# Vision-transformer block: attention's side work moved to other steps, and 56 expert units of 512 slots with gathered weights

## The reference

```python
def block(x, W, b, ...):
    h = patches(x) @ W + b                          # 64 images, 196 tokens of 192 (N = 12544)
    # attention, on layernorm(h): 12 heads of 16, rope, causal
    q, k, v = rope(heads(Wq)), rope(heads(Wk)), heads(Wv)
    weights = where(mask, erf(q k / 4) + 1, 0)
    h = h + (weights v / max(weights.sum(-1), 1e-6)) @ Wproj.T
    # experts, on flat = layernorm(h)
    probs = softmax(flat @ Wr)                       # 8 experts
    topk_p, topk_i = top_k(probs, 2), normalised
    order = argsort(-score, axis=1)[:, :3920]        # at most 3920 tokens per expert
    expert_out = (silu(d @ w1) * (d @ w3)) @ w2 * weight      # d = flat[order], inner 768
    routed = zeros.at[order].add(expert_out)
    shared = silu(flat @ s1) * (flat @ s3) @ s2      # all tokens
    return h + routed + shared
```

## Time and profile before

| what | us |
|---|---|
| median of three executions | 3905.7 |
| their range | 3896.83 to 3907.6 |
| profiled execution | 3916.64 |
| its span, first to last instruction | 3914.8 |
| TensorE busy | 3537.2 (90%) |
| VectorE busy | 2483.3 (63%) |
| ScalarE busy | 1703.8 (44%) |
| GpSimd busy | 1427.5 (36%) |
| mean granted TensorE clock (share of 2.4 GHz) | 0.848 |

### The profile page before, as it was taken

The page is one execution under the profiler, slowest core; times in us unless marked ns, Lnnn a source line. Parts: engine busy times, 40 slices in busy tenths (PEclk is TensorE's granted clock), DMA queues, the critical chain, the costliest instruction groups (busy, mean ns, idle before and its releaser), DMA issues. The chain is left out here.

```text
span 3914.8 us, 80584 instructions
## 1 busy us (share of the span) xinstructions
PE 3537.2 (90%) x28468; PEld 2523.2 (64%) x28468; DVE 2483.3 (63%) x4827; ACT 1703.8 (44%) x3390; POOL 1427.5 (36%) x1302
## 2 busy tenths in 40 slices
PE   6989889989999998998923999999999999999998
PEld 5766667767677676776712666666666666666665
DVE  5878778777787777877765555554444455345443
ACT  3444444444454444444401444434444444444443
POOL 1222222222222222222221555215555556555555
PEclk7877778777777777787555999999999999999999
DMA  1011111110110101101011222222332323323222
GB/s 67 31 47 39 39 51 34 43 51 26 51 49 28 51 31 46 51 31 47 24 49 48 63 70 71 67 75 35 61 62 39 60 37 62 62 36 61 39 39 32
DMA packets 166708, 186.21 MB, mean 48 GB/s; under 512 B 45263, under 2 KB 145711, under 8 KB 162319
## 3 DMA queue, kind: packets, MB, share of 16 engines
q1 hardware_dynamic: 95696, 123.03, 9.7%
q0 software_dynamic: 57472, 48.46, 8.3%
q10 hardware_dynamic: 13262, 10.65, 0.8%
HBM read 107.75 MB, written 67.85 MB: 45 GB/s over the span
## 5 line engine op out<-in xcount | busy, mean ns | idle before, releaser
L1235 DVE SCALAR_TENSOR_TENSOR ffn_hidden<-ffn_up,ffn_silu 128x490 f32<-128x490 f32 (+2 forms) x534 | 358.2, 672 | 803.9 <-ACT ffn_silu L1218 735.5
L656 POOL TENSOR_TENSOR weights<-weights,x_pair 128x400 f32<-128x400 f32 x384 | 395.6, 1030 | 1243.3 <-DVE weights L521 669.5
L1218 ACT ACTIVATE ffn_silu<-ffn_gate 128x490 f32<-128x490 f32 (+2 forms) x534 | 311.0, 583 | 700.8 <-PE ffn_up L1186 663.6
L570 DVE RECIPROCAL recip<-x_product 128x200 f32<-128x200 f32 x384 | 535.6, 1395 | 0.0
L1203 PE MATMUL ffn_out<-ffn_w_hi,ffn_hidden_hi 128*126 128x192 f16 (+2 forms) x2124 | 522.5, 246 | 0.0
L1205 PE MATMUL ffn_out<-ffn_w_hi,ffn_hidden_lo 128*126 128x192 f16 (+2 forms) x2124 | 522.4, 246 | 0.0
L1204 PE MATMUL ffn_out<-ffn_w_lo,ffn_hidden_hi 128*126 128x192 f16 (+2 forms) x2124 | 522.3, 246 | 0.0
L1391 POOL DMA_INDIRECT out_rows<-done,kept x256 | 426.6, 1666 | 153.7 <-issue 85.3
L1381 POOL DMA_INDIRECT tokens<-dram_x,ids x256 | 279.8, 1093 | 392.8 <-issue 228.5
L1228 DVE TENSOR_TENSOR ffn_hidden_lo<-ffn_hidden,ffn_hidden_hi 128x490 f16<-128x490 f32 (+2 forms) x534 | 355.4, 665 | 8.8
L740 PE MATMUL bank<-w_tok,patches 128*128 128x192 f32 x1536 | 346.1, 386 | 14.1 <-DVE ident L486 14.1
(11 more groups left out here) (185 smaller groups left out, 8074.4 us busy)
## 6 DMA issues: line engine op xcount, KB each, us to landing
patches<-in_patches SPq DMA_DIRECT2D x32, 1176.0 KB, 5.2
ffn_raw<-in_w SPq DMA_DIRECT2D x18, 768.0 KB
dram_x_t<-x_t SPq DMA_DIRECT2D x32, 392.0 KB, 2.5
x_t<-dram_x_t SPq DMA_DIRECT2D x24, 512.0 KB
base<-dram_h SPq DMA_DIRECT2D x24, 384.0 KB
out_rows<-sums ACTq DMA_DIRECT2D x24, 384.0 KB
v_held<-v SPq DMA_DIRECT2D x64, 102.0 KB, 2.3
dram_h<-h SPq DMA_DIRECT2D x32, 192.0 KB
```

What stands on the lines that cost most here:

```text
L570: nc.vector.reciprocal(recip[:, n % 2], x_product[:, n % 2]).then_inc(inverted, 1)
L656: nc.gpsimd.tensor_tensor(weights[:, n % 4], weights[:, n % 4], x_pair[:, n % 4, ::-1], ALU.mult)\
L1218: nc.scalar.activation(T.silu[:, m % 2, 0:n], T.gate[m % 2][:, 0:n], ACT.Silu, scale=1.0 / (TOKEN_SCALE * WEIGHT_SCALE)).then_inc(T.silued, 1)
L1235: nc.vector.scalar_tensor_tensor(T.hidden[:, m % 2, 0:n], T.up[m % 2][:, 0:n], HIDDEN_SCALE / (TOKEN_SCALE * WEIGHT_SCALE), T.silu[:, m % ...
```

## The change

The diff has two parts that don't touch.

**Attention.** TOK works two units ahead instead of one, with two buffers h_new: turn u makes the tokens of unit u+2. A first turn "pre" with TOK alone is added, and a turn "late" without TOK before the last two. Steps of the side work change (all engines), and the scores of the next unit's first pair move into step 11, ahead of attend. SP loads patches two units ahead, both at the start, and does the v_held copies ahead of the h2 and x2 stores.

**Experts.** A slot table of 56 units of 512, each with one expert: an expert's entries are rounded up to whole units at run time, so its unit count follows from the routing. A table `weights_of` gives each unit's expert. During the first 16 shared units of the loop (8 pairs) each expert's weights are loaded, split, and stored as half-precision rows in DRAM (`front`, 12,288 B per partition; `back`, 4,608 B). For each routed unit GpSimd gathers `front` and `back` by the unit's expert, double buffered.

```diff
-TOK, YT, PROJ, LN1T, QK, VV, X2T, ROUTE, QKT = (
-    (0, 1), (2, 3), (4, 5), (6, 7), (8, 9, 11, 12), (10, 13), (14, 15), (16,), tuple(range(17, 23)))
+LN1T, QK, VV, YT, PROJ, X2T, QKT, ROUTE, TOK = (
+    (0, 1), (2, 3, 4, 5), (6, 9), (7, 8), (10, 11), (13, 14), tuple(range(15, 21)), (22,), (12, 21))
...
# TensorE, attention
                 for n in range(PAIRS):
-                    if pairs:
-                        if n < PAIRS - 1:
-                            scores(kind, u, n + 1, qk_t[slot])
-                        if n >= LAG:
+                    if pairs and n < PAIRS - 1:
+                        scores(kind, u, n + 1, qk_t[slot])
+                    if n == PAIRS - 1 and has_next:
+                        copied(QKT)
+                        scores("first" if kind == "pro" else "mid", u + 1, 0, qk_t[prev])
+                    if pairs and n >= LAG:
...
+                    if n == 3 and has_next:
+                        pe.wait_ge(normed_ready, 4 * u + 8)
+                        transposed(LN1T, normed)
+                        copied(LN1T)
+                    if n in (3, 4) and has_next:
+                        for t in range(2 * n - 6, 2 * n - 4):
+                            out = room(QK[t])
...
+                    if n in (7, 8) and has_tokens:
...
+                        tokens(n - 7)
...
+                    if n == 10 and has_next:
+                        pe.wait_ge(roped, 4 * u + 8)
+                        for g in range(6):
+                            transpose_qk(g)
+                    if n == 11 and has_tokens:
+                        tokens(2)
+                        tokens(3)
+                    if n == 11 and has_prev:
+                        pos = X2T[0]
+                        pe.wait_ge(free[pos % NB], fills(kind, u, pos))
...
# VectorE, attention
+                    if n == 0 and has_next:
+                        norm(0, token_root(u - 1), h_new[prev], normed, normed_ready)
+                    if n == 1 and has_prev:
                         outputs(u - 1, 1)
...
-                    if n in (6, 7) and has_next:
+                    if n in (3, 4) and has_next:
...
+                    if n == 11 and has_tokens:
+                        dve.wait_ge(free[TOK[-1] % NB], fills(kind, u, TOK[-1]))
+                        nc.vector.tensor_tensor(h_new[slot][:], h_new[slot][:], over(bias[:], [128, 4, D]), ALU.add)\
+                          .then_inc(biased, 1)
+                        dve.wait_ge(biased, u + 3)
+                        spread_of(0, h_new[slot])
...
# routing
+            ts(rounded[:], offset[:, 1, E:2 * E], float(XU - 1), None, ALU.add)
+            ts(rounded[:], rounded[:], XU.bit_length() - 1, None, ALU.logical_shift_right)
+            step(nc.vector.tensor_copy(units[:], rounded[:]))
+            step(nc.vector.tensor_tensor_scan(ends[:], ones[:, 0:E], units[:], 0.0, ALU.mult, ALU.add))
...
# experts, SP
             def unit(g, half, slot, tiles, e=None):
...
+                if e is not None and slot == 0:
+
+                    sp.wait_ge(T.weights_lo, 3 * e + 6)
+                    sp.sem_inc(load_spacer, 1)
+                    sp.dma_start(dram["front"][bass.ds(e * 128, 128), :], T.front[1][:]).then_inc(staged, 16)
+                    sp.dma_start(dram["back"][bass.ds(e * 128, 128), :], T.back[1][:]).then_inc(staged, 16)
+                    load_weights(sp, dram, T, e + 1)
...
# experts, GpSimd
+            def routed(v, half, slot):
+                if not among(v, XUNITS - 1):
+
+                    pool.wait_ge(T.gated, MI * (SHARED + v))
+                    pool.sem_inc(spacer, 1)
+                    if not (isinstance(v, int) and v == 0):
+                        pool.wait_ge(back_in[slot], 16 * (half + slot))
+                        pool.sem_inc(spacer, 1)
+                    owned(v + 1, slot)
+                    weights(slot, "front", T.front[slot], front_in[slot])
...
+                nc.gpsimd.tensor_copy(kept[slot][:], ids[slot][:]).then_inc(ids_kept, 1)
...
                     gather(v + 2, half + 1, slot)
...
+                    pool.wait_ge(T.out_full, 2 * (SHARED + v))
+                    pool.sem_inc(spacer, 1)
+                    weights(slot, "back", T.back[slot], back_in[slot])
...
# experts, ScalarE, behind store(g - 1, ...)
+                if e is not None and slot == 1:
+
+                    act.wait_ge(staged, 32 * e + 32)
+                    act.wait_ge(T.raw_in, 48 * e + 96)
                     weights_hi(nc, T, 1)
...
# experts, VectorE
+        if m == 2 and between:
+            between()
...
+                def remainders():
+
+                    dve.wait_ge(T.weights_hi, 3 * e + 6)
+                    weights_lo(nc, T, 1)
```

More of the change, by code:

```diff
@@ L720, in transpose_qk, with tokens @@
                     last.then_inc(full[pos % NB], 1)
-                for n in range(PAIRS):
-                    if pairs:
-                        if n < PAIRS - 1:
-                            scores(kind, u, n + 1, qk_t[slot])
-                        if n >= LAG:
-                            if n == LAG:
-                                pe.wait_ge(held_in[slot], 32 if kind == "first" else 32 * (prior + 1 - slot) + 32)
-                            attend(kind, u, n - LAG, v[slot], v_held[slot])
+                def tokens(n):
+                    pos, at = TOK[n // 2], n % 2 * D
+                    out = room(pos) if n % 2 == 0 else bank[pos % NB]
+                    for i in range(KP):
+                        last = nc.tensor.matmul(out[:, at:at + D], wide(patches[slot], i, n), tok_w[:, i, :],
+                                                start=(i == 0), stop=(i == KP - 1))
+                    if n % 2:
+                        last.then_inc(full[pos % NB], 1)
@@ new lines, in turn @@
+                    if n in (3, 4) and has_next:
+                        for t in range(2 * n - 6, 2 * n - 4):
+                            out = room(QK[t])
+                            product(out[:, 0:2 * D], normed_t, t, qkv_w, 2 * D).then_inc(full[QK[t] % NB], 1)
+                    if n in (4, 5) and has_next:
+                        pos = VV[n - 4]
+                        out = room(pos)
+                        for c in range(2):
+                            last = product(out[:, c * D:(c + 1) * D], normed_t, 2 * (n - 4) + c, qkv_w[:, :, 2 * D:3 * D], D)
+                        last.then_inc(full[pos % NB], 1)
@@ L860, in routing @@
         rank = sb("rank", [128, E])
-        base = sb("base", [128, E])
+        ones = sb("ones", [128, 128])
+        row = sb("row", [128, 1])
+        numbers = sb("numbers", [128, XUNITS])
+        ended = sb("ended", [128, XUNITS, E])
+        owner = sb("owner", [128, XUNITS])
+        rounded = sb("rounded", [128, E], I32)
+        units = sb("units", [128, E])
+        ends = sb("ends", [128, E])
         place = sb("place", [128, E])
@@ L878, in routing @@
         block = ctx.enter_context(nc.Block())
-        constants = ((rank, "rank"), (same, "same"), (before, "before"), (base, "base"))
+        constants = ((rank, "rank"), (same, "same"), (before, "before"), (row, "row"), (numbers, "numbers"))
         @block.sync
@@ L1068, in _ @@
                 ts(slots[:, :, c], best[:], float(SLOTS), None, ALU.add)
+            tt(ended[:], numbers[:].unsqueeze(2).to_broadcast([128, XUNITS, E]),
+               ends[:].unsqueeze(1).to_broadcast([128, XUNITS, E]), ALU.is_ge)
+            step(nc.vector.tensor_reduce(owner[:], ended[:], AX.X, ALU.add))
+            ts(owner[:], owner[:], float(E - 1), None, ALU.min)
+            ts(weights_of[:], owner[:], 128.0, row[:, 0:1], ALU.mult, ALU.add)
 TOKEN_SCALE, WEIGHT_SCALE, HIDDEN_SCALE = 2.0 ** 6, 2.0 ** 6, 2.0 ** 4
```

468 lines of the change are left out of this document (221 added, 247 removed).

## The result

The changed kernel takes 3965.1 us (median of four runs, 3960.68 to 3972.31), against 3901.3 us for the kernel before in the runs beside it. The ratio is 1.017, 95% interval 1.013 to 1.021: it is slower, by 1.7%. The forecast was 3752 us and a range to 3925, so both miss. The profiled execution has a span of 3958.8 us, 44.0 more than before.

A forecast was written before the change was run, and what follows sets the result against it. TensorE was taken as bound in attention, shared and routed units, GpSimd close behind in the last. From 3916.6: attention -180, routing +4, shared +150, short unit -8, routed -120 give 3763, less 10.9 for the median: 3752 us; range 3600 to 3925.

The forecast's parts named there:

- the ids load beside the weights: Routed units, GpSimd's loop: the ids load takes 0.6 us more beside weights, in a loop of 19.7 us.
- rival E: Routed units: GpSimd's loop replaces TensorE as bound, 26 us by dearer weight gathers and later ids; 4050 us, chance 0.12.
- The point of decision of rival E: Routed units: the time per unit from which rival E decides, 23.4 us.
- The x_t term with its clock: Shared units: tokens queued behind 4.3 MB on SP's queue cost 11.5 us per pair, the low clock afterwards 2 us.
- the casts, the remainders and their clock: Shared units with preparation: TensorE loses 2.1 us per pair to ScalarE's casts and 3.2 to VectorE's remainders.
- Rival D: Shared units: SP's queue doesn't hold the tokens, so 13.5 us less for each of 8 pairs; 3644 us, chance 0.12.
- The short unit: End of shared stage: the one preparation beside the short unit goes, saving 8 us.
- Waits: Attention: TensorE's waits of 4.3 us per turn go, as the start of the softmax chain is covered.
- Clock: Attention: 2.0 us less per turn, as 24 token matmuls at the boundary replace idle time.
- The cover of the boundary: Attention, step 11: next turn's scores ahead of attend, with 24 token matmuls and route matmul behind, cover the softmax chain's start.
- Rivals B and C: Attention: B, clock stays high, 48.6 us per turn, 3590, chance 0.15; C, heavy run stays low, 58, 3870, chance 0.15.
- Routing: Routing stage: a memset, a second small matmul, some twelve small VectorE operations and the owner table add 4 us.

The follow-up runs named there:

- thin_front: Changed kernel with the front gather of units 3 to 54 cut to an eighth of its row, 1536 B of 12,288; 3818 us in a single run.
- front_later: Changed kernel with the front gather issued behind the token gather instead of ahead of the ids load; 4088 us, ratio 1.045 to the kernel before.
- xt_on_scalar_queue: Changed kernel with the x_t load behind a weight preparation issued by ScalarE on its own queue; 3966 us in a single run.
- xt_ahead: Changed kernel with each shared unit's x_t load issued one unit earlier, before the stores and raw loads; 3890 us, ratio 0.995 to the kernel before.
- casts_spread: Changed kernel with ids loaded once, x_t loads before stores, last token matmuls in step 9, remainders and casts one behind each m; 3651 us, ratio 0.931.
- tokens_nine: Changed kernel with the last 24 token matmuls of a turn in step 9 instead of step 11; 3949 us, ratio 1.012 to the kernel before.
- both_ahead: Changed kernel with ids of all units loaded once and x_t loads ahead of the stores; 3700 us, ratio 0.949 to the kernel before.

## Why the prediction failed

**Routed units, the step that failed.** The sum had 0.6 us for the ids load beside the weights, from a row in which it took 4.02 us instead of 3.42 beside raw weights, and ended at 19.7 us per loop. It measured 7.02 us. The windows of before show what that row was worth. The raw load was issued at 2598.19 us and this ids load at 2606.33, when the DMA engines had under two us of it left (the DMA share is the last column but one: 0.86, then 0.03):

```profile
2604.00:2606.00 2.00, 1.94 (x16) 1.40 (x13) 0.85 (x3) 0.70 (x3) 1.69 (x3) 0.88 1.02 331
2606.00:2608.00 2.00, 1.95 (x20) 1.96 (x21) 1.24 (x4) 1.50 (x4) 0.23 (x2) 1.00 0.86 214
2608.00:2610.00 2.00, 2.00 (x27) 2.00 (x25) 1.32 (x2) 0.61 (x2) 0.00 (x0) 1.00 0.03 1
```

In the changed kernel the ids load is issued at 3023.38 us, with nearly the whole front gather ahead of it:

```profile
3024.00:3026.00 2.00, 2.00 (x26) 1.92 (x24) 0.00 (x0) 0.00 (x0) 0.00 (x0) 1.00 0.80 301
3026.00:3028.00 2.00, 0.14 (x2) 0.00 (x0) 0.00 (x0) 0.73 (x2) 0.00 (x0) 1.00 0.90 375
3028.00:3030.00 2.00, 0.72 (x2) 0.28 (x3) 0.00 (x0) 0.00 (x0) 0.00 (x0) 0.62 0.12 38
```

So a row of the tail of a transfer was taken for the price of the whole. With it GpSimd's loop, 23.75 us and not 19.7, took the place of TensorE's 20.16 us as the bound of the stage. The right number stood in rival E ("ids 3 us later behind the weights' packets") and was argued away with "ids and weights use different queues". `thin_front` and `front_later` show the front gather's transfer as the cause, and `xt_on_scalar_queue` that another queue doesn't help. Rival E's mechanism is the one that came, by one of its three terms; the forecast gave it 0.12.

**The rest of the loop was sized right.** The second weight gather costs 1.30 us (1.4 forecast), the first one lies almost in the landing wait (2.79 for 2.02), a gather of 12,288 B rows holds GpSimd for 1.09 us (1.17 in the mean from 2700 to 3700 us), little more than one of 768 B rows at 1.02 (rival E had it at twice that). The point of decision of rival E, 23.4 us per unit, held too: at 23.6 the whole is just slower. E's 26 us was too much. TensorE's own bound of 20.16 us was right: with the ids wait gone the unit takes 20.17.

**Shared units: the right number for half a wrong reason.** +139 against +142. The two intervals of a pair are 36.2 and 19.8, 18.1 us above two plain units, for 18.8 forecast. The x_t term with its clock, 13.5 us forecast, is 10.9 by `xt_ahead` (a pair falls from 55.9 to 45.0 us). What is left above two plain units there, 7.2 us, is the casts, the remainders and their clock, for 5.3 forecast; `casts_spread` takes all but 0.7 of it away. The errors cancelled. Of the reason given for x_t the late issue holds (SP's wait for the remainders), and the order on SP's queue is there too, but it is not what the time hangs on: on a queue of its own the load lands no sooner. The bytes were in the sum and gave the time. Rival D falls. The short unit gave back 4.2 us (from its own first token remainder to the first routed one 23.7 us before, 19.5 now), not 8.

**Attention.** 54.1 us per turn forecast, 54.8 measured, so -165 instead of -188 for 30 turns; the rest of the gap is in the start and the last three turns, +23 instead of +8 (the first logits copy alone comes 26 us later). The near hit of the turn is in part luck. Waits: 4.3 us were to go, and TensorE's idle time fell by 2.5; the 4.3 had counted in the wait on the last qk_t copy (18.9 of the 85.5 us), which stayed. Clock: 2.0 us were taken, and TensorE's busy time fell by 3.0. The cover of the boundary: wrongly named, as `tokens_nine` shows. Granted clock: forecast 0.75 to 0.80, measured 0.82 here and 0.79 to 0.81 in the other kernels with this code. Rivals B and C fall. The section "HAM oscillation — how this bites in real kernels" of the Trainium skill's "TensorE: Matmul & The Clock Gate" blames idle gaps for the low clock; here the gaps mostly went (busy 91% to 95% from 400 to 1600 us) and the clock rose from 0.76 to 0.82, but not to 1, so it is part of the story and not the whole, as the stretch of the earlier trace rows already said.

**Routing** came out within 2 us.

**Small slips in the sums.** Behind casts of 3.91 us with 1.6 us of room the silu is 2.3 us late and not 2.9; 1176 KB at 381 GB/s are 3.2 us and not 4; rival E's terms give 26.4 us per unit, so 4071 us. Together the first two move the forecast by under 6 us.

## What to carry to other kernels

When a change adds large transfers, look for every small load that an in-order engine waits for, whatever its queue, and price it with the bytes that are in flight beside it: 1.57 MB turned a wait of 3.3 us for 4 KB into one of 7.0 us here, once per unit, on a loop that had 1.1 us of room before the change. The cure is not to move the large transfer, which may be on the path itself, but to take the small one out of the loop (one load of all indices) or to issue it a step early. And work inserted into a pipeline of small steps belongs one piece behind each step: the same preparation cost 7 to 8 us per pair as two lumps (`xt_ahead`, `both_ahead`) and under 1 us spread.

## What the runs showed of the hardware that I had not expected

- A load on a queue of its own, beside others that fill the DMA engines (412 GB/s), landed no sooner: 8.0 to 10.2 us against 8.7 to 8.9 on the queue of the others (12.6 once), and 3.7 ahead of any preparation.
- A 4 KB load started its first packet 3.9 us after its issue beside a 1.57 MB gather of another queue, and 0.9 us after it with the gather issued later.
- An indirect gather's time on GpSimd hardly depends on the row: in the mean 1.17 us for 128 rows of 12,288 B, 1.10 for rows of 1536 B in `thin_front`, 1.02 for token rows of 768 B.
- The granted clock of the same attention code differed between the kernels and chips that ran it, 0.79 to 0.82 from 400 to 1600 us, and the turn with it, 57.0 to 54.8 us. The four kernels that ran on one of the chips have 0.79 to 0.80, three on another 0.81. Over 30 turns that is 66 us, more than many an edit is worth, and it may be why the attention part measured 119 us alone and 141 in the first pair of traces; no run shows that.
